# Read stage and multiply stage of a decoder layer merged into one block, with new orders on VectorE and ScalarE

## The chip, the cores and the metric

One core of a Trainium2 chip runs the whole layer. The metric is the device time of one execution in microseconds (us); three executions are shown, with their median. The engines are TensorE (PE, its weight loads PEld), VectorE (DVE), ScalarE (ACT), GpSimd (POOL) and the DMA queue of SyncE (SP).

## The reference, cut to what matters

The layer adds three parts to a state `x` of 2 x 512 tokens by 1024: a rotary attention with 4-bit weights, a "read, attend, read, multiply, write" part whose state has 4 channels for each of 256 features, and a linear layer with 4-bit weights from a table. The change lies in the second part:

```python
hidden_states = rat_write(hidden_states, attn_out, ...)      # first write
mlp_in = rat_read(hidden_states, mlp_read_w, mlp_read_g, mlp_read_b, 2)
g_in, u_in = (mlp_in[..., :H], mlp_in[..., H:])
gate = jnp.einsum('bli,oi->blo', g_in, mlp_in_w[0])
up = jnp.einsum('bli,oi->blo', u_in, mlp_in_w[1])
mlp_out = jax.nn.silu(gate) * up
hidden_states = rat_write(hidden_states, mlp_out, ...)       # second write

# rat_read: y = einsum(x, W) over the 4 channels, for each of the outputs; then a
#   normalisation over the 256 features, times gamma, plus beta
# rat_write, last line: hs * A_full + out * B_full, with
#   A_bar = exp(delta * A_neg), B_bar = (A_bar - 1) / (A_neg - SSM_EPS) * B_proj
```

## The kernel before, in words

The 1024 tokens are eight tiles of 128 (`NT` = 8), four of each batch. Nothing schedules the work but the order in which each engine's list of instructions is written, and semaphores between the engines. A block begins on all engines when the block before has ended on all of them.

`write_read` (L1990) is one block. In its first part TensorE and ScalarE make the low-rank products of the first write, while VectorE finishes the dequantiser's quarters up to `Q_MLP`. Its second part, called the **read loop** here, goes over the tiles i = 0 to 7, and each engine has its own list:

- VectorE, for tile i: `wr.update(i)` (three instructions, L1695, L1699, L1702, that make the two terms of the next state), then `rd.stats(i-1)` (mean and variance of the former tile's read, L899 and L902), then `wr.total(i)` (L1708, the sum that is the next state of the tile), at i = 2 the four instructions of `soft_sum`, then `rate(i+2)` (L1676), `skip(i+1)` (L1684) and `rd.finish(i-1)` (four small instructions from the root to the scale, L820 to L823, and two that normalise, L911).
- TensorE, for tile i: waits for `wr.new` (the end of `total(i)`), `turn_h` (eight transposes of the new state, L864), `products` (sixteen small matmuls, as profiled, on its copy in SBUF, L875), `turn_y(i-1)` (transposes of the normalised former tile, L892), and for i under 4 half a tile of the dequantised weight (`turn_half`, L1972).
- ScalarE, for tile i: `exponent(i+1)` (L1659), `root(i-1)` (L924), `copy_y(i-2)` (L930), `copy_h(i)` (two copies, L920), `copy_half` (L1982). Exponential, square root and SiLU each need another function table on ScalarE; the loads stand in the list as ACT_TABLE_LOAD under the line of the instruction that wants them.

`mlp` (its code is L1711 to L1755) is a block of its own. It has 16 steps, one for each batch and each of the 8 tiles of 128 of M. A **step** on TensorE is eight matmuls of 128x512 (four to the gate, four to `up`, L1733), on ScalarE one SiLU (L1745), on VectorE one product (L1753). Three pairs of PSUM buffers go round: step n waits for the product of step n-3. With each step go one **quarter** of the dequantiser on ScalarE (`blend`, two ACTIVATEs, L1887) and on VectorE (`merge`, L1855 to L1897), 16 quarters in all. Ahead of step 9, TensorE turns one tile of the weight in two halves (`deq.turn`, L1972), and the second waits for ScalarE's copy of the first. `write_norm_forward` is the block behind it: the second write, a normalisation and the linear layer.

Of the kernel before, what the change touches and what calls it, by code (L numbers as in the profile page):

```python
# [15 lines left out]
P = 128  # L16
# [809 lines left out]
class Read:  # L826


    def __init__(self, nc, ctx, name, h, rw, gam, bet, n_out, ident, eps, half_mask, inT, p_h, p_y, p_t, hT=None, yn=None,
# [7 lines left out]
        self.hT = hT or [sb(f"{name}hT{i}", [P, D])[:] for i in range(2)]  # L837
# [29 lines left out]
    def products(self, pe, i):  # L867
        W, ny = self.W, len(self.p_y)
        if i == 0:
            pe.wait_ge(self.made, 1)  # L870
        pe.wait_ge(self.hc, 2 * i + 2)
        if i >= ny:
            pe.wait_ge(self.yn_done, self.n_out * (i - ny + 1))
        for k in range(KT):
            ins = pe.matmul(self.p_y[i % ny][:, k // 4, (k % 4) * W:(k % 4 + 1) * W],  # L875
                            self.hT[i % 2][:, k * P:(k + 1) * P], self.wbd[:, k].rearrange("p o j -> p (o j)"),
                            start=True, stop=True)
        ins.then_inc(self.ydone, 1)
# [36 lines left out]
    def copy_h(self, act, i):  # L915
        for g in range(2):
# [3 lines left out]
            act.activation(self.hT[i % 2][:, g * 512:(g + 1) * 512], self.p_h[g][:], ACT.Copy).then_inc(self.hc, 1)  # L920
# [57 lines left out]
def read_attend(nc, a, acc, ident, ident_bf, ident_r, eps, h, mask, half_mask, ones, deq, loads, early, pos, inv, qkvT, swapT,  # L978
# [4 lines left out]
    with ExitStack() as ctx:  # L983
        sb, psum, sem = scope(nc, ctx)
        with ExitStack() as lease:
# [20 lines left out]
                  hT=[wide[:, n * D:(n + 1) * D] for n in range(2)], lent=lent,  # L1006
# [547 lines left out]

class Write:
# [33 lines left out]
    def main(self, pe, i):  # L1589
# [4 lines left out]
        for k in range(self.n_k):  # L1594
            lhs = self.sT[:, i % 2, k, :] if self.src is not None else self.srcT[:, k, i * P:(i + 1) * P]
# [115 lines left out]
def mlp(nc, inT, wT, yT, deq, fT):  # L1711

    with ExitStack() as ctx:
        sb, psum, sem = scope(nc, ctx)
        sg = [sb(f"m_sg{i}", [P, S]) for i in range(2)]
        p_g = [psum(f"m_g{i}", [P, S]) for i in range(3)]
        p_u = [psum(f"m_u{i}", [P, S]) for i in range(3)]
        done, silu, mul = sem("m_done"), sem("m_silu"), sem("m_mul")
        p_w = psum("m_pw", [P, 512])
        block = ctx.enter_context(nc.Block())  # L1720
        steps = [(b, m) for b in range(B) for m in range(MT)]
        turn_at = {9: 4}

        @block.tensor
        def _(pe):
            for n, (b, m) in enumerate(steps):
                if n in turn_at:
                    deq.turn(pe, turn_at[n], p_w)
                if n >= 3:
                    pe.wait_ge(mul, n - 2)  # L1730
                for g, dst in enumerate((p_g, p_u)):
                    for ic in range(IC):
                        ins = pe.matmul(dst[n % 3][:], wT[:, g, ic, m * P:(m + 1) * P],  # L1733
                                        inT[:, g * IC + ic, b * S:(b + 1) * S], start=ic == 0, stop=ic == IC - 1)
                ins.then_inc(done, 1)

        @block.scalar
        def _(act):
            for n in range(len(steps)):
                if n in turn_at:  # L1740
                    deq.copy(act, turn_at[n], p_w, fT)
                act.wait_ge(done, n + 1)
                if n >= 2:
                    act.wait_ge(mul, n - 1)
                act.activation(sg[n % 2][:], p_g[n % 3][:], ACT.Silu).then_inc(silu, 1)  # L1745
                for q in range(mlp_quarter(n), mlp_quarter(n + 1)):
                    deq.blend(act, q)

        @block.vector
        def _(dve):  # L1750
            for n, (b, m) in enumerate(steps):
                dve.wait_ge(silu, n + 1)
                dve.tensor_tensor(yT[:, m, b * S:(b + 1) * S], p_u[n % 3][:], sg[n % 2][:], ALU.mult).then_inc(mul, 1)  # L1753
                for q in range(mlp_quarter(n), mlp_quarter(n + 1)):
                    deq.merge(dve, q)  # L1755


# [28 lines left out]

def mlp_quarter(n):

    return Q_MLP + (Q_W2 - Q_MLP) * n // (2 * MT)


class Dequantiser:
# [152 lines left out]
    def merge(self, dve, q):  # L1945

        h, pair = q // QUARTERS, q % QUARTERS
        if pair == 0:
# [41 lines left out]
def write_read(nc, h, o_all, odT, bias_row, du, rw, gam, bet, ones, ident, eps, half_mask, inT, spread, fT, deq, fetch, early):  # L1990


    with ExitStack() as ctx:
        sb, psum, sem = scope(nc, ctx)
        p_h = [psum(f"w1ph{i}", [P, 512]) for i in range(2)]
        p_y = [psum(f"w1py{i}", [P, 2, 512]) for i in range(2)]
        p_t = [psum(f"w1pt{i}", [P, 512]) for i in range(2)]
        ab = [spread[:, n * 3 * XH:(n + 1) * 3 * XH].rearrange("p (n c) -> p n c", c=3) for n in range(2)]
        bb = [spread[:, (2 + n) * XC * XH:(3 + n) * XC * XH].rearrange("p (n c) -> p n c", c=XC) for n in range(2)]
        wr = Write(nc, ctx, "w1", h, ident, ones, odT, bias_row, du, IC, 2, [t[:] for t in p_h],  # L2000
                   [p_y[0][:, n] for n in range(2)], p_t[0], src=o_all, p_s=[p_y[1][:, n] for n in range(2)], ab=ab, bb=bb)
        rd = Read(nc, ctx, "r2", h, rw, gam, bet, 2, ident, eps, half_mask, inT, p_h, p_y, p_t,
                  hT=[spread[:, (4 + n) * D:(5 + n) * D] for n in range(2)])
        p_w = p_t[1]
        flat = wr.sp[:].rearrange("p t s -> p (t s)")
        deq.borrow(Q_W1, [flat[:, n * HALF:(n + 1) * HALF] for n in range(4)]
                   + [inT[:, n // 2, HALF * (n % 2):HALF * (n % 2 + 1)] for n in range(6)])
        chain, fetched, first = sem("w1chain"), sem("w1fetched"), sem("w1first")
        half = NT // 2
# [16 lines left out]
        def _(pe):  # L2026
            wr.turn(pe, 0)
# [13 lines left out]
            for i in range(NT + 1):  # L2041
                if i < NT:
                    pe.wait_ge(wr.new, i + 1)
                    rd.turn_h(pe, i)
                    rd.products(pe, i)
                if i >= 1:
                    rd.turn_y(pe, i - 1)
                if i < len(W1_HALVES):
                    deq.turn_half(pe, W1_HALVES[i], p_w)

        @block.scalar
        def _(act):
            for b in range(B):
# [18 lines left out]
            for i in range(NT + 2):  # L2072
# [4 lines left out]
                if 1 <= i <= NT:  # L2077
                    rd.root(act, i - 1)
                if i >= 2:
                    rd.copy_y(act, i - 2)  # L2080
                if i < NT:
                    rd.copy_h(act, i)
                if 1 <= i <= len(W1_HALVES):
                    deq.copy_half(act, W1_HALVES[i - 1], p_w, fT)

        @block.vector
        def _(dve):
            link = Chain(dve, chain)
            for q in range(Q_W1, Q_MLP):
# [6 lines left out]
            for i in range(NT + 1):  # L2096
                if i < NT:
                    wr.update(dve, i)
                if i >= 1:
                    rd.stats(dve, link, i - 1)  # L2100
                if i < NT:
                    wr.total(dve, i)
                    if i + 2 == half:
                        wr.soft_sum(dve, link, 1)
                    if i + 2 < NT:
# [3 lines left out]
                if i >= 1:  # L2109
                    rd.finish(dve, link, i - 1)  # L2110


def write_norm_forward(nc, h, acc, x1_kept, odT, bias_row, du, ones, ident, eps, fT, bias_src, out, deq):
# [3 lines left out]
    with ExitStack() as ctx:  # L2117
# [5 lines left out]
                   [t[:] for t in po[2:4]], p_l, srcT=acc)  # L2123
# [36 lines left out]
        def _(pe):  # L2160
# [11 lines left out]
            def unit(u):  # L2172
# [7 lines left out]
                for k in range(KT):  # L2180
                    ins = pe.matmul(po[u % 4][:], acc[:, k, i * P:(i + 1) * P], fT[:, k, g * 512:(g + 1) * 512],  # L2181
# [20 lines left out]
        def _(act):  # L2202
# [11 lines left out]
            def copy_z(i):  # L2214
# [141 lines left out]
def program(nc, a, out):  # L2356
    with ExitStack() as keep:
# [24 lines left out]
        with ExitStack() as ml:  # L2382
            sbm, _, _ = scope(nc, ml)
            wT, inT2 = sbm("mlp_w", [P, 2, IC, M]), sbm("inT2", [P, 2 * IC, TOK])
            with ExitStack() as w1:
                sbw, _, _ = scope(nc, w1)
                odT1, bias1, du1 = sbw("odT1", [P, IC, OD]), sbw("bias1", [1, OD - C_B]), sbw("du1", [DR + 1, XH])
                spread = acc[:, 0:6, :].rearrange("p k t -> p (k t)")
                write_read(nc, h, o_all, odT1, bias1, du1, rw2, g2, b2, ones, ident, eps, half_mask, inT2, spread, fT, deq,
# [3 lines left out]
            deq.use(Q_MLP, "dm_", ml, nc)  # L2393
            mlp(nc, inT2, wT, acc, deq, fT)
# [65 lines left out]
```

## Time and profile before

| | |
|---|---|
| median of 3 executions | 1802.5 us (1802.19 to 1802.68) |
| the profiled execution, its own time | 1804.03 us |
| its span, first to last instruction | 1802.3 us |
| busy in the span: PE, DVE, ACT, POOL | 89%, 75%, 51%, 32% |
| mean granted TensorE clock | 0.941 |
| read loop (first update of a tile to the end of the block) | 1466.8 to 1546.7 us |
| `mlp` block | 1546.7 to 1611.3 us |

The profiled execution spends 1.7 us outside its span. The shares of busy time are means over stages that have different limits; the stages that are changed are 145 us of the 1802, so only what happens between 1466 and 1611 us is read in detail. A granted clock of 0.50 is the lower of TensorE's two levels (1.2 GHz), 1.00 is the upper (2.4 GHz).

### The profile page before, as it was taken

The page shows a single profiled execution, that of the slowest core. Times are in us where ns is not written, and L with a number is a line of the kernel's source. Part 1 is how long each engine was busy: PE and PEld are TensorE (multiplying, and loading weights), DVE is VectorE, ACT ScalarE, POOL GpSimd, SP SyncE. Part 2 cuts the span into 40 slices and gives each one's busy share as a digit, 9 for nine tenths or more (in the row PEclk, how much of TensorE's full clock was granted, in tenths as well). Part 3 has the DMA queues.
Part 4 walks back from the last instruction along what each step waited for, and adds up shares of the span by engine and source line. Part 5 has one row for each costly group of instructions (what it writes and reads, how often), then busy time and mean ns, then how long its engine had stood idle before and what let it go on. Part 6 is the DMA issues. An engine that isn't in the chain of part 4 may idle for free. (4 is left out here: it accounts for less than half of the span.)

```text
span 1802.3 us, 21041 instructions
## 1 busy us (share of the span) xinstructions
PE 1595.5 (89%) x6880; PEld 1056.0 (59%) x6880; DVE 1358.9 (75%) x2078; ACT 910.2 (51%) x1682; POOL 577.8 (32%) x463
## 2 busy tenths in 40 slices
PE   4899999999999999999999988677889757888999
PEld 3466666666666666666666655465456446445444
DVE  7688788788878888888887866685578679568881
ACT  3345455555454454554555444233468876457630
POOL 2246446446446446455455454201110100000000
PEclk9999999999999999999999999887889865899999
DMA  5002102102101111111110010230644200010121
GB/s 182 24 25 59 35 24 59 36 24 59 36 25 58 35 33 51 35 37 46 36 45 26 24 35 12 79 140 30 123 84 58 91 1 0 1 35 1 47 76 41
DMA packets 30963, 84.20 MB, mean 47 GB/s; under 512 B 6006, under 2 KB 7304, under 8 KB 30600
## 3 DMA queue, kind: packets, MB, share of 16 engines
q1 hardware_dynamic: 30856, 82.87, 16.0%
q8 instruction: 56, 0.92, 0.2%
q14 instruction: 51, 0.42, 0.1%
HBM read 70.27 MB, written 12.58 MB: 46 GB/s over the span
## 5 line engine op out<-in xcount | busy, mean ns | idle before, releaser
L518 DVE SCALAR_TENSOR_TENSOR acc<-pj,sc_o,acc 128x1024 f32<-128x1024 f32 x232 | 293.8, 1278 | 89.6 <-PE pj L649 86.2
L628 POOL TENSOR_TENSOR prob<-prob,inv_total 128x512 f32<-128x512 f32 (+3 forms) x256 | 189.6, 745 | 386.0 <-DVE inv_total L560 386.0
L518 DVE SCALAR_TENSOR_TENSOR q_acc<-pj,sc_q,q_acc 128x1024 f32<-128x1024 f32 x224 | 286.2, 1278 | 34.6 <-PE pj L649 29.3
L649 PE MATMUL pj<-ctx_hi,w_o 128*128 128x512 f32 x528 | 237.1, 449 | 25.6 <-ACT spare L407 12.3
L649 PE MATMUL pj<-zT_hi,w_q 128*128 128x512 f32 x512 | 225.9, 441 | 3.7 <-PEq L81 3.1
L649 PE MATMUL pj<-ctx_lo,w_o 128*128 128x512 f32 x528 | 208.1, 394 | 0.0
L461 ACT ACTIVATE prob<-ps,low_max 128x512 f32<-128x512 f32 (+3 forms) x256 | 134.0, 526 | 144.4 <-DVE low_max L553 144.3
L649 PE MATMUL pj<-zT_lo,w_q 128*128 128x512 f32 x512 | 204.9, 400 | 0.0
L703 PE MATMUL ps<-kT,qT 128*128 128x512 f32 (+3 forms) x512 | 186.2, 446 | 10.2 <-ACT prob L461 10.2
L727 PE MATMUL pv<-probT,v 128*128 128x512 f32 (+3 forms) x512 | 169.4, 433 | 0.0
L649 PEld LDWEIGHTS pj<-ctx_hi,w_o 128*128 128x128 f32 x528 | 99.1, 188 | 110.6 <-DVE acc L518 43.0
L451 ACT ACTIVATE probT<-pt 128x512 f32<-128x512 f32 (+3 forms) x256 | 111.4, 435 | 69.5 <-PE pt L717 68.5
L553 DVE TENSOR_REDUCE low_max<-ps 128x1 f32<-128x512 f32 (+3 forms) x256 | 123.1, 481 | 28.2 <-PE ps L706 28.2
L717 PE MATMUL pt<-ident,prob 128*128 128x128 f32 x640 | 115.6, 279 | 19.0 <-ACT probT L451 9.4
L618 POOL TENSOR_TENSOR acc<-acc,spare 128x1024 f32<-128x1024 f32 x32 | 76.6, 2394 | 143.9 <-ACT spare L407 143.9
L649 PEld LDWEIGHTS pj<-zT_hi,w_q 128*128 128x128 f32 x512 | 98.2, 192 | 40.7 <-issue 21.1
L649 PE MATMUL pj<-zT_hi,w_kv 128*128 128x512 f32 x240 | 119.8, 499 | 1.8 <-DVE kv_acc L518 1.1
L703 PEld LDWEIGHTS ps<-kT,qT 128*128 128x128 f32 x512 | 94.0, 191 | 46.6 <-ACT prob L461 27.4
L717 PEld LDWEIGHTS pt<-ident,prob 128*128 128x128 f32 x640 | 74.4, 141 | 77.8 <-POOL prob L628 42.2
L2181 PE MATMUL w2po<-fT,acc 128*128 128x512 f32 x256 | 112.8, 599 | 2.2 <-ACT acc L2221 2.2
L649 PEld LDWEIGHTS pj<-ctx_lo,w_o 128*128 128x128 f32 x528 | 99.6, 189 | 16.6
L407 ACT ACTIVATE spare<-pj,sc_o 128x1024 f32<-128x1024 f32 x32 | 35.7, 1115 | 144.8 <-PE pj L649 144.8
(332 smaller groups left out, 3154.9 us busy)
## 6 DMA issues: line engine op xcount, KB each, us to landing
raw_o<-in_w_o SPq DMA_DIRECT2D x33, 512.0 KB, 3.6
raw_q<-in_w_q SPq DMA_DIRECT2D x32, 512.0 KB, 3.6
x_ring<-qk_kept SPq DMA_DIRECT2D x64, 128.0 KB, 4.7
ln_x<-in_x SPq DMA_DIRECT2D x8, 512.0 KB, 7.1
raw_kv<-in_w_k SPq DMA_DIRECT2D x8, 512.0 KB, 3.5
raw_kv<-in_w_v SPq DMA_DIRECT2D x8, 512.0 KB, 4.6
x<-in_x SPq DMA_DIRECT2D x8, 512.0 KB, 7.2
x_kept<-x SPq DMA_DIRECT2D x8, 512.0 KB, 3.5
```

Source lines behind the costliest of these rows:

```text
L407: act.activation(dst[:], pj[slot][:], ACT.Copy, scale=scale).then_inc(evac_s, 1)
L451: act.activation(probT[:, b, 0:qt + 1, qt * P:(qt + 1) * P], pt[:, 0:(qt + 1) * P].rearrange("p (k c) -> p k c", c=P), ACT.Copy).then_inc( ...
L461: act.activation(prob[:, k % PROBS, 0:w], ps[n % 2][:, 0:w], ACT.Exp, bias=low_max[:, n:n + 1], scale=-1.0, accum_out=total[:, n:n + 1]).t ...
L518: dve.scalar_tensor_tensor(out=dst, in0=pj[slot][:], scalar=scale, in1=dst, op0=ALU.mult, op1=ALU.add).then_inc(evac_v, 1)
L553: dve.tensor_reduce(low_max[:, n:n + 1], ps[n % 2][:, 0:(qt + 1) * P], AX.X, ALU.min).then_inc(max_done, 1)
L618: pool.tensor_tensor(acc[:, n, :], acc[:, n, :], spare[:], ALU.add).then_inc(spare_added, 1)
L628: pool.tensor_tensor(prob[:, k % PROBS, 0:w], prob[:, k % PROBS, 0:w], inv_total[:, n:n + 1].to_broadcast([P, w]), ALU.mult).then_inc(norm ...
L649: ins = pe.matmul(pj[slot][:, b * S:(b + 1) * S], lhs, part[:, b * S:(b + 1) * S], start=n == 0, stop=n == 1)
L703: pe.matmul(ps[n % 2][:, 0:w], qT[:, b * S + qt * P:b * S + (qt + 1) * P], kT[:, par, b * S:b * S + w], start=True, stop=False)
L717: ins = pe.transpose(pt[:, c * P:(c + 1) * P], prob[:, k % PROBS, c * P:(c + 1) * P], ident[:])
L727: ins = pe.matmul(pv[:, c * P:S], v[:, par, b * S + c * P:b * S + (c + 1) * P], probT[:, b, c, c * P:S], start=c == 0, stop=c == QT - 1)
L2181: ins = pe.matmul(po[u % 4][:], acc[:, k, i * P:(i + 1) * P], fT[:, k, g * 512:(g + 1) * 512], start=k == 0, stop=k == KT - 1)
```

## The change

1. The block `mlp` goes; its 16 steps move into the block of `write_read`.
2. Steps 0 to 3 stand inside the read loop. TensorE has step i-5 for i = 5 to 8, behind `products(i)` and ahead of `turn_y(i-1)`; ScalarE has its SiLU (`gated`) for i = 6 to 9, behind `root`; VectorE has the product at the end of i = 6, 7, 8, and that of step 3 after the loop. These four steps share one pair of PSUM buffers (`p_g`, `p_u`), so step n waits there for the product of step n-1. Steps 4 to 15 come after the loop with three pairs, two of which are the buffers of `turn_h` and `products`.
3. VectorE's list in the read loop: `total(i)` now ahead of `stats(i-1)`. ScalarE's list: `copy_y(i-2)`, `copy_h(i)`, then `root(i-1)`.
4. The dequantiser: quarter `Q_MLP` is done at the end of the read loop (`begin` and `merge(..., begun=True)` on VectorE, one `blend` on ScalarE), the other 15 with steps 4 to 15, two of them with steps 7, 11 and 15. The turn of a weight tile stands ahead of step 12, not of 9.
5. Places in SBUF and PSUM: the two buffers of the products are one bank each, the transposed state lies in a part of `fT` that is free, the working tiles of the dequantiser are borrowed, and `acc` holds the multiply stage's output by batch, with batch 1 first; later readers of it are changed alike (`by_batch`, `turned_tile`).

```diff
+def by_batch(acc):
+    return acc[:].rearrange("p (b x) (y s) -> p b (x y) s", b=B, s=S)
+def turned_tile(v, k, i):
+    return v[:, B - 1 - i // (NT // B), k, (i % (NT // B)) * P:(i % (NT // B) + 1) * P]
...
-def mlp(nc, inT, wT, yT, deq, fT):
...
+MLP_IN_READ, MLP_FROM = 4, 5
+STEPS = [(b, m) for b in range(B) for m in range(MT)]
+MLP_TURNS = {12: 4}
 def mlp_quarter(n):
-    return Q_MLP + (Q_W2 - Q_MLP) * n // (2 * MT)
+    return Q_MLP + 1 + (Q_W2 - Q_MLP - 1) * (n - MLP_IN_READ) // (len(STEPS) - MLP_IN_READ)
...
+    def begin(self, dve, h):
+        self.low_shift(dve, h)
+        self.low_bit(dve, h)
+        for n in range(3):
+            self.high_bit(dve, h, n)
...
+        p_g, p_u = psum("m_g", [P, S]), psum("m_u", [P, S])
+        gate, up = (p_g, p_h[0], p_y[0]), (p_u, p_h[1], p_y[1])
...
         @block.tensor
+            def step(n):
+                b, m = STEPS[n]
+                pe.wait_ge(rd.yc, rd.nb * NT * (b + 1) // B)
+                if n == 0:
+                    pe.wait_ge(fetched, 16 * len(fetch))
+                    pe.wait_ge(wr.dc, NT)
+                if n == MLP_IN_READ:
+                    pe.wait_ge(rd.hc, 2 * NT)
+                elif n == MLP_IN_READ + 1:
+                    pe.wait_ge(rd.yn_done, rd.n_out * NT)
+                elif n:
+                    pe.wait_ge(mul, n if n < MLP_IN_READ else n - 2)
+                k = 0 if n < MLP_IN_READ else n % 3
+                for g, dst in enumerate((gate, up)):
+                    for ic in range(IC):
+                        ins = pe.matmul(dst[k][:], wT[:, g, ic, m * P:(m + 1) * P],
+                                        inT[:, g * IC + ic, b * S:(b + 1) * S], start=ic == 0, stop=ic == IC - 1)
+                ins.then_inc(done, 1)
...
                     rd.products(pe, i)
+                if i >= MLP_FROM:
+                    step(i - MLP_FROM)
                 if i >= 1:
                     rd.turn_y(pe, i - 1)
                 if i < len(W1_HALVES):
                     deq.turn_half(pe, W1_HALVES[i], p_w)
+            for n in range(MLP_IN_READ, len(STEPS)):
+                if n in MLP_TURNS:
+                    deq.turn(pe, MLP_TURNS[n], p_w)
+                step(n)
...
         @block.scalar
+            def gated(n):
+                act.wait_ge(done, n + 1)
+                if n == 0:
+                    act.wait_ge(wr.mul_done, half)
+                if n >= 2:
+                    act.wait_ge(mul, n - 1)
+                act.activation(sg[n % 2], gate[0 if n < MLP_IN_READ else n % 3][:], ACT.Silu).then_inc(silu, 1)
...
-                if 1 <= i <= NT:
-                    rd.root(act, i - 1)
                 if i >= 2:
                     rd.copy_y(act, i - 2)
                 if i < NT:
                     rd.copy_h(act, i)
+                if 1 <= i <= NT:
+                    rd.root(act, i - 1)
+                if i > MLP_FROM:
+                    gated(i - 1 - MLP_FROM)
                 if 1 <= i <= len(W1_HALVES):
                     deq.copy_half(act, W1_HALVES[i - 1], p_w, fT)
+                if i == NT:
+                    deq.blend(act, Q_MLP)
+            for n in range(MLP_IN_READ, len(STEPS)):
+                if n in MLP_TURNS:
+                    deq.copy(act, MLP_TURNS[n], p_w, fT)
+                gated(n)
+                for q in range(mlp_quarter(n), mlp_quarter(n + 1)):
+                    deq.blend(act, q)
...
         @block.vector
+            def product(n):
+                b, m = STEPS[n]
+                if n == 0:
+                    dve.wait_ge(wr.st, NT)
+                if n == MT:
+                    dve.wait_ge(wr.new, NT)
+                dve.wait_ge(silu, n + 1)
+                dve.tensor_tensor(yT[:, B - 1 - b, m, :], up[0 if n < MLP_IN_READ else n % 3][:], sg[n % 2],
+                                  ALU.mult).then_inc(mul, 1)
...
             for i in range(NT + 1):
                 if i < NT:
                     wr.update(dve, i)
-                if i >= 1:
-                    rd.stats(dve, link, i - 1)
+                if i == NT:
+                    dve.wait_ge(wr.new, NT)
+                    deq.begin(dve, Q_MLP // QUARTERS)
                 if i < NT:
                     wr.total(dve, i)
                     if i + 2 == half:
                         wr.soft_sum(dve, link, 1)
+                if i >= 1:
+                    rd.stats(dve, link, i - 1)
+                if i < NT:
                     if i + 2 < NT:
                         wr.rate(dve, i + 2)
                     if i + 1 < NT:
                         wr.skip(dve, i + 1)
                 if i >= 1:
                     rd.finish(dve, link, i - 1)
+                if i > MLP_FROM:
+                    product(i - 1 - MLP_FROM)
+            deq.merge(dve, Q_MLP, begun=True)
+            product(MLP_IN_READ - 1)
+            for n in range(MLP_IN_READ, len(STEPS)):
+                product(n)
+                for q in range(mlp_quarter(n), mlp_quarter(n + 1)):
+                    deq.merge(dve, q)
```

## Rows read from the trace of the kernel before

**Rows 1.** Busy time by stretch: length, PE, PEld, DVE, ACT, POOL, clock, DMA.

```profile
1510.40:1519.00 8.60, 6.52 (x29) 5.70 (x28) 7.87 (x17) 6.78 (x11) 0.00 (x0) 0.50 0.01 2
1562.00:1579.20 17.20, 17.20 (x41) 7.41 (x39) 12.93 (x21) 10.00 (x15) 0.00 (x0) 1.00 0.00 0
```

**Rows 2.** Waits in the read loop: us in total, times, longest us.

```profile
PE w1ph L864 <- DVE h L1708: 19.9, 8, 10.3
ACT r2sd L924 <- DVE r2mv L902: 17.9, 8, 4.8
```

**Rows 3.** VectorE's timeline in the read loop: start us, us, instruction, idle before.

```profile
1468.55 1.22 DVE L1702 TENSOR_TENSOR acc<-acc,w1od 128x1024 f32<-128x1024 f32 x1
1469.87 1.23 DVE L1708 TENSOR_TENSOR h<-h,acc 128x1024 f32<-128x1024 f32 x1
...
1506.24 0.76 DVE L899 BATCH_NORM_STATS2 r2st<-w1py 128x6 f32<-128x256 f32 x2 [0.52 <-PE w1py L875]
...
1507.20 1.19 DVE L1708 TENSOR_TENSOR h<-h,acc 128x1024 f32<-128x1024 f32 x1
...
1509.63 0.16 DVE L820 RECIPROCAL r2r<-r2sd 128x2 f32<-128x2 f32 x1
...
1510.44 0.99 DVE L911 TENSOR_SCALAR r2yn<-w1py,r2mv,r2t 128x256 f32<-128x256 f32 x2
1511.36 0.95 DVE L1695 SCALAR_TENSOR_TENSOR acc<-acc,w1nb 128x768 f32<-128x768 f32 x1
...
1514.82 0.76 DVE L899 BATCH_NORM_STATS2 r2st<-w1py 128x6 f32<-128x256 f32 x2 [0.51 <-PE w1py L875]
```

**Rows 4.** ScalarE's timeline in the read loop, tiles 5 and 6.

```profile
1511.56 1.28 ACT L1659 ACT_TABLE_LOAD   x1
1512.86 0.84 ACT L1659 ACTIVATE acc<-acc 128x768 f32<-128x768 f32 x1
...
1515.90 0.29 ACT L924 ACTIVATE r2sd<-r2mv,eps 128x2 f32<-128x2 f32 x1 [0.90 <-DVE r2mv L902]
1516.10 1.49 ACT L930 ACTIVATE inT<-w1pt,b,g 128x128 f32<-128x128 f32 x4
...
1519.03 0.60 ACT L920 ACTIVATE acc<-w1ph 128x512 f32<-128x512 f32 x1 [0.26 <-PE w1ph L864]
```

**Rows 5.** ScalarE's timeline in the block after `mlp`.

```profile
1675.92 0.39 ACT L1633 ACTIVATE w2od<-w2po 128x256 f32<-128x256 f32 x1 [0.78 <-PE w2po L1610]
1676.33 1.28 ACT L2205 ACT_TABLE_LOAD   x1
```

**Rows 6.** TensorE's timeline in the read loop and in `mlp`.

```profile
1517.03 1.97 PE L864 MATMUL w1ph<-ident,h 128*128 128x128 f32 x8 [1.39 <-DVE h L1708]
...
1523.15 1.06 PE L892 MATMUL w1pt<-ident,r2yn 128*128 128x128 f32 x4
...
1546.75 3.43 PE L1733 MATMUL m_g<-inT,mlp_w 128*128 128x512 f32 x4 [1.85 <-PEq L1993]
...
1551.73 1.88 PE L1733 MATMUL m_g<-inT,mlp_w 128*128 128x512 f32 x4
...
1562.03 1.88 PE L1733 MATMUL m_g<-inT,mlp_w 128*128 128x512 f32 x4
...
1577.48 1.88 PE L1733 MATMUL m_u<-inT,mlp_w 128*128 128x512 f32 x4
...
1582.43 1.88 PE L1733 MATMUL m_g<-inT,mlp_w 128*128 128x512 f32 x4
```

**Rows 7.** ScalarE's and VectorE's timelines behind the last step.

```profile
1606.66 0.60 ACT L1745 ACTIVATE m_sg<-m_g 128x512 f32<-128x512 f32 x1 [1.43 <-PE m_u L1733]
1607.16 1.51 ACT L1887 ACTIVATE dm_t<-dm_t,d_lut,d_step 128x512 f32<-128x512 int32 x2
...
1607.29 0.69 DVE L1753 TENSOR_TENSOR acc<-m_u,m_sg 128x512 f32<-128x512 f32 x1 [1.29 <-ACT m_sg L1745]
...
1610.28 0.73 DVE L1897 COPY_PREDICATED d_w<-dm_t 128x512 f32<-128x512 int32 x1
```

More of the change, by code:

```diff
@@ L836, in __init__ @@
         self.wbd = sb(name + "wbd", [P, KT, n_out, 32])
-        self.hT = hT or [sb(f"{name}hT{i}", [P, D])[:] for i in range(2)]
+        self.hT = hT or [sb(f"{name}hT{i}", [P, 2, 512])[:] for i in range(2)]
         self.yn = yn or [sb(f"{name}yn{i}", [P, n_out * XH])[:] for i in range(2)]
@@ L1708, in total @@
         dve.tensor_tensor(hv, hv, self.bb[i % 2], ALU.add).then_inc(self.new, 1)
-def mlp(nc, inT, wT, yT, deq, fT):
[L1713 to L1755, printed above, removed]
 HALF = D // 2
@@ L1943, in merge_one, with merge @@
             self.keep_all(dve, h)
-    def merge(self, dve, q):
+    def begin(self, dve, h):
[3 more added lines that the diff above has]
+            self.high_bit(dve, h, n)
+    def merge(self, dve, q, begun=False):
         h, pair = q // QUARTERS, q % QUARTERS
-        if pair == 0:
+        if pair == 0 and not begun:
             if q in STAGES:
@@ L1987, in copy, with write_read @@
             self.copy_half(act, 2 * o + g, pt, fT)
-def write_read(nc, h, o_all, odT, bias_row, du, rw, gam, bet, ones, ident, eps, half_mask, inT, spread, fT, deq, fetch, early):
+def write_read(nc, h, o_all, odT, bias_row, du, rw, gam, bet, ones, ident, eps, half_mask, inT, acc, wT, fT, deq, fetch, early):
     with ExitStack() as ctx:
         sb, psum, sem = scope(nc, ctx)
+        spread = acc[:, 0:4, :].rearrange("p k t -> p (k t)")
         p_h = [psum(f"w1ph{i}", [P, 512]) for i in range(2)]
-        p_y = [psum(f"w1py{i}", [P, 2, 512]) for i in range(2)]
-        p_t = [psum(f"w1pt{i}", [P, 512]) for i in range(2)]
+        p_y = [psum(f"w1py{i}", [P, 512]) for i in range(2)]
+        p_t, p_w = psum("w1pt", [P, 512]), psum("w1pw", [P, 512])
+        p_g, p_u = psum("m_g", [P, S]), psum("m_u", [P, S])
@@ L2005, in write_read @@
+        gate, up = (p_g, p_h[0], p_y[0]), (p_u, p_h[1], p_y[1])
+        yT = by_batch(acc)
         flat = wr.sp[:].rearrange("p t s -> p (t s)")
+        old = wr.od[:].rearrange("p t s -> p (t s)")
+        sg = [old[:, n * S:(n + 1) * S] for n in range(2)]
         deq.borrow(Q_W1, [flat[:, n * HALF:(n + 1) * HALF] for n in range(4)]
                    + [inT[:, n // 2, HALF * (n % 2):HALF * (n % 2 + 1)] for n in range(6)])
+        deq.borrow(Q_MLP, [flat[:, n * HALF:(n + 1) * HALF] for n in range(4)]
+                   + [old[:, n * HALF:(n + 1) * HALF] for n in range(2, 8)])
@@ L2008, in write_read @@
         chain, fetched, first = sem("w1chain"), sem("w1fetched"), sem("w1first")
+        done, silu, mul = sem("m_done"), sem("m_silu"), sem("m_mul")
         half = NT // 2
```

30 lines of the change are left out of this document (14 added, 16 removed).

## The prediction, made before the changed kernel was run

> **What bounds the kernel now.** The page's busy shares say TensorE (89%), but they are means; the change touches only the read loop and the multiply block, so I read the busy time by stretch there first. It shows two regimes. In the read loop VectorE is the busy engine (7.87 of 8.60 us), ScalarE has 6.78, and TensorE, at the lower clock, still has 2.1 us idle in each tile. In the multiply block TensorE is busy without a gap at the upper clock [rows 1]. So moving steps from the second stage into the gaps of the first looks like a gain. Four steps are worth 3.43 us each at the upper clock: 10.30 us for three, 1551.73 to 1562.03 [rows 6].
>
> Second, the waits in the read loop: TensorE waits for the new state of a tile (19.9 us), and ScalarE's root waits for the statistics (17.9 us) [rows 2]. Third, VectorE's timeline gives the loop's period: statistics start at 1506.24 and again at 1514.82, so 8.58 us, of which only 0.51 are idle and end with TensorE's products [rows 3]. The ring that ends last is: sum of the next state, transposes, copy by ScalarE, products, statistics, next sum.
>
> **The change: the order in the read loop.** With the sum ahead of the statistics the ring above is cut, and VectorE's own list is left. Its pieces, start to start, are [rows 3]: statistics 0.96 (1506.24 to 1507.20); sum, rate and skip 2.43 (to 1509.63); reciprocal to normalising 0.81; normalising 0.92 (to 1511.36); update 2.95 (to 1514.31, where the idle 0.51 begins). Together 8.07. Add 0.10, because the sum now stands right behind the multiply that it needs (1468.55 + 1.22 = 1469.77 against 1469.87). That would be 8.17 us a tile, a gain of 0.4.
>
> But the reciprocal needs the root, and the root now stands behind `copy_h(i)` on ScalarE. The second copy begins 2.00 us after the transposes of its tile and lasts 0.60 (1517.03 and 1519.03) [rows 4, 6]. Then the root's function table has to be loaded, as the exponential has used ScalarE since. Before, this 1.28 us load stood right behind the exponential, in ScalarE's idle time. Is it put directly ahead of its user, or moved up by whoever places it? The next block answers: ScalarE there was idle 0.78 us, waiting for a copy's input, and the square root's load came only behind that copy (1675.92, 1676.33) [rows 5]. I take it that the same holds here: load 1.28, gap 0.02, root 0.29 [rows 4].
>
> So the new ring, from one tile's transposes to the next: copies 2.60, load 1.30, root and hand-over 0.35, to the normalising 0.81, 0.92, update and gap 3.05, sum 1.19, and 0.06 to the transposes: **10.28 us against 8.58**. The new state is early only in name: it is made behind `finish` of the former tile, which is late by the load. Tiles 3 to 4 and 4 to 5 lose 1.70 each. At the first tiles I take 0.4 in all, between nothing and 1.7 each: VectorE waited 2.3 us for the first products there, and at tile 2 the four instructions of `soft_sum` cover the load. Tile 5's transposes come at 1517.03 + 3.8 = 1520.8.
>
> A rule of the Trainium skill speaks against this part, in "ScalarE: Activation LUTs", sections "What ACT_TABLE_LOAD costs" and "Table sets: the hidden batching unit": calls are to be grouped by table set, and each switch is to be budgeted at some 2.66 us, a load of 1283 ns and a drain of 1380 ns. The trace agrees on the load alone: it ends at 1512.84, and the exponential starts at 1512.86 [rows 4]. By the page's drain the six loads that I find exposed below would add an estimated 8 us more to the sum; I go by the row.
>
> **Steps 0 to 3 inside the loop.** What does a step take there? At the start of `mlp` the first gate group of four matmuls took 3.43 us at the lower clock, and the next step began 4.98 us after the first [rows 6]. Steps at the upper clock take 3.43, a whole step at the lower clock would be twice the first group, 6.9. The read loop ran at 0.50 throughout [rows 1], so each step begins low; I take 5.0 and keep 3.4 and 6.9 as bounds.
>
> Round 5 (tile 5's transposes to tile 6's): transposes and products occupy TensorE for 6.12 (1517.03 to 1523.15), step 0 5.0, `turn_y` 0.86 (an estimate: its 1.06 less the overlap with what follows): 12.0. The ring's 10.28 lies inside it.
>
> Round 6: `turn_y(4)` stood behind the step, so ScalarE's `copy_y(4)` (1.49) comes now, ahead of `copy_h(6)`; the copies end 2.75 after the transposes began. Load of the root's table to 4.05, root to 4.38, table load for SiLU to 5.68, SiLU 0.60, product 0.69 [rows 7] to 7.05. Only then may step 1 start, as the four steps share one pair of buffers: TensorE has been through with its products since about 6.4. Step 5.0, `turn_y` 0.86: 12.9.
>
> The last round has tile 7 and, behind it, the end of the loop. Step 2 again starts at 7.05 and ends at 12.05, `turn_y(6)` is done at 13.1, and only then do `copy_y(6)`, the load, root 7, the load for SiLU, SiLU and the product follow one another: 1.5 + 1.3 + 0.3 + 1.3 + 0.6 + 0.7 = 5.7, with hand-overs 18.95. Step 3 and `turn_y(7)`: 24.8. Queued behind root 7 on VectorE are `finish(7)`, the product and quarter `Q_MLP`; `begin` of that quarter fits in the wait.
>
> So step 4 starts at 1520.8 + 12.0 + 12.9 + 24.8 = 1570.5. Before, it started at 1562.03 [rows 6]: **+8.5**. The six exposed loads are those of rounds 3 and 4, two in round 6, two at the end; that of round 5 lies beside the step.
>
> **Steps 4 to 15.** Twelve at 3.43 as before: nothing. VectorE now has 15 quarters in twelve steps. A quarter and its product took VectorE 12.93 us busy in five steps [rows 1], 2.6 a step; 15/12 of the quarters keep it under 3.43, and three buffers bridge the double ones. If that cover fails, each double costs up to 1.4. The turn ahead of step 12 comes behind step 11, which has two quarters on ScalarE: TensorE's second half waits for a copy behind four blends, not two. The turn cost 3.23 before (1577.48 to 1582.43 less 1.72); two blends more are 1.4 (1.51 less an overlap) [rows 6, 7]: **+1.4**, between 0 and 3. The last step too has two quarters instead of one; behind it the block ended 4.35 us after the SiLU's start (1606.66 to 1611.01), now two blends later: **+1.4**.
>
> **At nothing:** the block boundary before `mlp` goes, but what it held, `turn_y` and the copy, is counted above. No DMA is moved; SP's and GpSimd's lists keep their place. The new places in `acc`, `fT` and PSUM keep every instruction's shape. The later readers of `acc` only step by 512 instead of 1024 elements; I know no row for that, bounds 0 and 0.5.
>
> **Sum:** 8.5 + 1.4 + 1.4 = +11.3. The profiled execution has 1804.0 (span 1802.3 and 1.7 around), so it would be 1815.3. The median of the runs is 1.5 lower: **1813.8 us**, slower by 0.6%. About 0.2%, 3.6 us, is what the measurement can tell from no change.
>
> **Rivals.**
> - *TensorE stays at the lower clock through steps 0 to 3.* For it: 0.50 throughout a loop in which TensorE was busy three quarters of the time. Against it: the dense matmuls raised it within one group at 1546.75. Each step has 1.9 more, and step 4 starts low: 4 x 1.9 + 1.6 = +9: 1823.
> - *The clock rises with step 0 and stays.* Steps at 3.43, round 5 then limited by the ring at 10.3, rounds 6 and last 11.1 and 20.9 by the same sum: step 4 at 1563.1, +1.0, with the two 1.4 1806.3. For it: TensorE's gaps shrink. Against it: it idles before each step for the SiLU.
> - *The table load is moved up ahead of the copies.* The ring is then 8.98, with the root still behind `copy_h`, and the loads in round 6 and at the end vanish: step 4 at about 1560, 1803.4, no difference. Against it: [rows 5].
> - *The steps fit into the shadow* (the other side). If step, SiLU and product lay wholly beside the ring, tile "8" would be reached at 1520.8 + 3 x 10.28 = 1551.6, 10.4 us before the old start of step 4, and with 2.8 given back the time is 1794.9. It decides when the three rounds take less than 38.4 us together, not 49.7. Against it: the shared pair of buffers and `turn_y` behind the step.
>
> **How the numbers follow.** Forecast (steps partly low) 0.57; all low 0.16; clock stays up 0.12; load moved up 0.08; shadow 0.07. 1806.3 sits near the bound, so half of that case counts as no change: faster 0.07, same 0.13, slower 0.80. The range leaves out the shadow, the load and a part beyond the lower clock's case: 1804 to 1823.
>
> **What would show it.** In the profile after: the root's table load behind L920's copies, with VectorE's reciprocal idle some 2 us for ScalarE in each of tiles 3 to 5, and transposes 10.3 apart; TensorE idle before steps 1 to 3, the longest before step 3 (some 6 us); step 4 at about 1570; a stall of 4.6 us at the turn; the next block at about 1622. Wrong would be: transposes 8.2 to 8.6 apart (the load hidden), steps of 3.4 or 6.9 us in the loop, or step 4 before 1562.

## The result and the profile after

The changed kernel takes 1814.2 us (median of 4 executions, 1812.09 to 1815.37) against 1802.59 before: ratio 1.0055, 95% interval 1.0037 to 1.0073. It is slower by 0.6%; 1813.8 was forecast. In a second comparison (e9) the same two kernels gave 1819.1 and 1803.36, ratio 1.0074 (1.0054 to 1.0093).

The profiled execution took 1813.46 us (span 1811.8). I measure from the first transposes of the read loop, those of tile 0, as the stages ahead of them, which the change leaves alone, end at different times: first transposes at 1471.15 us before, 1467.40 after, and between 1465.24 and 1475.88 in all fourteen profiles of this study. This is TensorE's timeline after, with its transposes at L864 and its steps at L2025; it answers to [rows 6]:

```profile
1467.40 1.97 PE L864 MATMUL w1ph<-ident,h 128*128 128x128 f32 x8 [10.28 <-DVE h L1718]
...
1506.99 1.97 PE L864 MATMUL w1ph<-ident,h 128*128 128x128 f32 x8 [2.23 <-DVE h L1718]
...
1517.27 1.97 PE L864 MATMUL w1ph<-ident,h 128*128 128x128 f32 x8 [3.08 <-DVE h L1718]
1519.92 3.67 PE L875 MATMUL w1py<-r2wbd,fT 128*128 128x64 f32 x16 [0.69 <-ACT fT L920]
1523.39 2.93 PE L2025 MATMUL m_g<-inT,mlp_w 128*128 128x512 f32 x4
1526.16 1.88 PE L2025 MATMUL m_u<-inT,mlp_w 128*128 128x512 f32 x4
1527.88 0.60 PE L892 MATMUL w1pt<-ident,r2yn 128*128 128x128 f32 x4
1528.31 1.04 PE L864 MATMUL w1ph<-ident,h 128*128 128x128 f32 x8
...
1535.45 3.74 PE L2025 MATMUL m_g<-inT,mlp_w 128*128 128x512 f32 x4 [1.76 <-DVE acc L2123]
...
1541.18 1.04 PE L864 MATMUL w1ph<-ident,h 128*128 128x128 f32 x8
...
1548.25 3.75 PE L2025 MATMUL m_g<-inT,mlp_w 128*128 128x512 f32 x4 [2.34 <-DVE acc L2123]
1551.80 2.33 PE L2025 MATMUL m_u<-inT,mlp_w 128*128 128x512 f32 x4
1553.97 0.60 PE L892 MATMUL w1pt<-ident,r2yn 128*128 128x128 f32 x4
1560.52 3.75 PE L2025 MATMUL m_g<-inT,mlp_w 128*128 128x512 f32 x4 [5.95 <-DVE acc L2123]
1564.06 3.02 PE L2025 MATMUL m_u<-inT,mlp_w 128*128 128x512 f32 x4
1566.92 0.60 PE L892 MATMUL w1pt<-ident,r2yn 128*128 128x128 f32 x4
1567.36 3.60 PE L2025 MATMUL w1ph<-inT,mlp_w 128*128 128x512 f32 x8
...
1591.39 3.60 PE L2025 MATMUL w1py<-inT,mlp_w 128*128 128x512 f32 x8
1594.83 0.60 PE L1946 MATMUL w1pw<-ident,d_w 128*128 128x128 f32 x4
1598.97 0.66 PE L1946 MATMUL w1pw<-ident,d_w 128*128 128x128 f32 x4 [3.55 <-ACT fT L1956]
1599.47 1.88 PE L2025 MATMUL m_g<-inT,mlp_w 128*128 128x512 f32 x4
...
1619.48 7.72 PE L1606 MATMUL w2po<-odT,acc 128*128 128x376 f32 x16 [6.12 <-PEq L1967]
```

Read down the starts of L864: 1506.99 to 1517.27 is tile 4, 10.28 us. Then come the four steps, each with a wait for VectorE's product ahead of it but the first: 1.76 us before step 1, 2.34 before step 2, 5.95 before step 3. Step 4 begins at 1567.36.

ScalarE in tile 4, and at the end of the loop; it answers to [rows 4]:

```profile
1508.99 0.60 ACT L920 ACTIVATE fT<-w1ph 128x512 f32<-128x512 f32 x1 [0.26 <-PE w1ph L864]
1509.61 1.28 ACT L924 ACT_TABLE_LOAD   x1
1510.90 0.29 ACT L924 ACTIVATE r2sd<-r2mv,eps 128x2 f32<-128x2 f32 x1
...
1554.61 1.50 ACT L930 ACTIVATE inT<-w1pt,b,g 128x128 f32<-128x128 f32 x4 [7.22 <-PE w1pt L892]
1556.13 1.28 ACT L924 ACT_TABLE_LOAD   x1
1557.42 0.29 ACT L924 ACTIVATE r2sd<-r2mv,eps 128x2 f32<-128x2 f32 x1
1557.74 1.28 ACT L2067 ACT_TABLE_LOAD   x1
1559.03 0.60 ACT L2067 ACTIVATE w1od<-m_g 128x512 f32<-128x512 f32 x1
```

The load stands between copy and root. VectorE waits for the root. Its timeline in tile 4, and at the end of the loop (normalising, then the product of step 2):

```profile
1511.23 0.17 DVE L820 RECIPROCAL r2r<-r2sd 128x2 f32<-128x2 f32 x1 [1.98 <-ACT r2sd L924]
...
1558.78 0.99 DVE L911 TENSOR_SCALAR r2yn<-w1py,r2mv,r2t 128x256 f32<-128x256 f32 x2 [0.27 <-DVE r2t L823]
1559.69 0.68 DVE L2123 TENSOR_TENSOR acc<-m_u,w1od 128x512 f32<-128x512 f32 x1
```

The waits between 1466 and 1568 us:

```profile
ACT inT L930 <- PE w1pt L892: 27.9, 8, 7.2
DVE r2r L820 <- ACT r2sd L924: 22.9, 7, 5.8
...
PE m_g L2025 <- DVE acc L2123: 10.1, 3, 6.0
```

Against [rows 2] the wait has turned round: ScalarE's root waited 17.9 us in all for VectorE's statistics, now VectorE waits 22.9 for the root.

### The profile page after: what moved, and what is told of

It is laid out like the page before. It is cut to its first block and busy times, and to the rows that moved or that the text cites. A ratio compares the mean times of both kernels' runs of the same rounds, so it can differ in the third digit from the quotient of the medians.

```text
span 1811.8 us, 21054 instructions
## 1 busy us (share of the span) xinstructions
PE 1594.8 (88%) x6880; PEld 1052.9 (58%) x6880; DVE 1358.0 (75%) x2078; ACT 915.6 (51%) x1686; POOL 578.8 (32%) x463
## 5 line engine op out<-in xcount | busy, mean ns | idle before, releaser
L649 PEld LDWEIGHTS pj<-ctx_lo,w_o 128*128 128x128 f32 x528 | 99.6, 189 | 16.4
```

The costliest lines, as they stand in the source:

```text
L649: ins = pe.matmul(pj[slot][:, b * S:(b + 1) * S], lhs, part[:, b * S:(b + 1) * S], start=n == 0, stop=n == 1)
```

## The experiments

Twelve kernels ran. Single executions scatter by several us on those chips (the kernel before: most between 1798 and 1811), and the ratios compare with the kernel before only, so each experiment is compared with the changed kernel by its profile: "stretch" is the time from the first transposes to the start of the next block, "tile 5" and "step 4" are counted from the first transposes too. Each stretch is that of one execution. Two kernels were profiled twice: the changed one differed by 1.5 us (e9), the best one by 0.2 (e11), so a difference under some 1.5 us is not told apart here.

| kernel | tile 5 | tile 6 | tile 7 | step 4 | stretch | median us | ratio to before (95%) |
|---|---|---|---|---|---|---|---|
| before | 45.88 | 54.45 | 63.02 | 90.88 | 140.18 | 1802.59 | |
| changed | 49.87 | 60.91 | 73.78 | 99.96 | 152.08 | 1814.2 | 1.0055 (1.0037 to 1.0073) |
| e1 root first | 43.17 | 56.32 | 67.23 | 90.22 | 144.04 | 1806.99 | 1.0021 (1.0000 to 1.0043) |
| e2 old orders | 45.29 | 55.73 | 67.77 | 89.00 | 142.81 | 1811.48 | 1.0030 (1.0014 to 1.0046) |
| e3 preload | 45.62 | 57.04 | 69.37 | 90.91 | 144.72 | 1809.64 | 1.0030 (1.0011 to 1.0048) |
| e4 orders only | 49.68 | 59.96 | 70.24 | | 147.45 | 1811.32 | 1.0027 (1.0008 to 1.0046) |
| e5 turn_y first | 49.87 | 60.82 | 72.77 | 89.19 | 143.95 | 1808.28 | 1.0027 (1.0009 to 1.0044) |
| e6 even quarters | 49.88 | 61.19 | 74.18 | 100.46 | 147.41 | 1811.06 | 1.0040 (1.0024 to 1.0056) |
| e7 no SiLU | 49.87 | 60.99 | 73.74 | 94.68 | 148.48 | 1813.5 | 1.0049 (1.0034 to 1.0064) |
| e8 best | 45.87 | 57.19 | 66.60 | 82.83 | 129.78 | 1795.33 | 0.9938 (0.9918 to 0.9958) |
| e9 changed again | 49.71 | 61.66 | 74.98 | 101.51 | 153.63 | 1819.1 | 1.0074 (1.0054 to 1.0093) |
| e10 before, turn split | 45.88 | 54.46 | 63.04 | 90.93 | 139.14 | 1803.24 | 0.9999 (0.9987 to 1.0011) |
| e11 best again | 45.90 | 57.40 | 66.82 | 83.06 | 130.01 | 1793.45 | 0.9942 (0.9920 to 0.9964) |
| e12 best, sum first | 43.14 | 56.38 | 65.06 | 83.12 | 130.08 | 1792.56 | 0.9929 (0.9913 to 0.9946) |

**e1, the root first.**

```diff
+                if 1 <= i <= NT:
+                    rd.root(act, i - 1)
                 if i >= 2:
                     rd.copy_y(act, i - 2)
                 if i < NT:
                     rd.copy_h(act, i)
-                if 1 <= i <= NT:
-                    rd.root(act, i - 1)
```

> Of the changed kernel, only ScalarE's list in the read loop is put back: the root of the former tile ahead of the two copies; VectorE keeps the sum ahead of the statistics, the steps stay in the loop. My theory (the root with its table load behind the copies sets the ring): VectorE no longer waits 2 us for the root; but the copies of a tile now come behind root and copy_y, some 1.3 us late, so TensorE's list (transposes, late products, turn_y, half turn) limits tiles 3 and 4 to 9.2 and 8.4 us; the product of step 0 and 1 comes 1.5 us earlier, that of step 2 some 3 us; in all about -9 us on the changed kernel, 1805. Rival (the steps in the loop alone set the time, the lists do not matter): 1814, no difference from the changed kernel. Rival (late copies cost as much as the load): 1811 to 1814.

The stretch fell by 8.0 us. Tile 5 came 6.7 sooner, tile 5 to 6 took 13.2 instead of 11.0: the late copies exist, but cost less than the root's place. VectorE, no longer waiting, began its sums 8.17 and 8.18 us apart (1490.78, 1498.95, 1507.13), where the prediction had put its own list at 8.17.

**e2, both lists old.** e1's edit, and `rd.stats(dve, link, i - 1)` ahead of `wr.total(dve, i)` again.

> The changed kernel with both lists put back (VectorE: statistics ahead of the sum; ScalarE: root ahead of the copies); the steps, the turn and the quarters stay as changed. My theory: transposes 8.6 us apart up to tile 5 as before the change, then steps as in the changed kernel with the product earlier: about -8.5 us, 1805.5, still some 3 us slower than before the change, which is the price of the steps' place and of the double quarters. Rival (moving the steps is what costs, the orders are free): 1813 to 1814. Rival (moving the steps is a gain and only the orders hide it): under 1799.

The stretch fell by 9.3 us, so the orders are not free, and the steps with the rest of the change are still 2.6 us dearer than before it. Step 4 came 1.9 us sooner than before the change; what is behind it gave that back and more (see e6).

**e3, the load alone.** The sharpest test: nothing is taken away, one tiny instruction per tile is added (`warm` is a new tile for its unused result).

```diff
+                if 1 <= i <= NT:
+                    act.activation(warm[:, i:i + 1], eps[:], ACT.Sqrt)
                 if i >= 2:
                     rd.copy_y(act, i - 2)
```

> The changed kernel with one more instruction per tile: a square root of one element per partition on ScalarE, directly ahead of copy_y and copy_h, its result unused. It changes nothing but where the root's table load stands. My theory (the load behind the copies costs 1.3 us in each tile that it is exposed in): transposes of tiles 3 to 5 come 9.0 us apart instead of 10.3, and six exposed loads less in all: -7.8 us, 1806.5. Rival (the root's place behind the copies costs, not the load): 1813 to 1815. Rival (VectorE's list is the bound anyway): 1813 to 1815.

ScalarE's timeline of e3, from the end of tile 4 (its transposes began at 1503.15) to the root in tile 5 (1512.02):

```profile
1508.60 1.28 ACT L2095 ACT_TABLE_LOAD   x1
1509.90 0.20 ACT L2095 ACTIVATE warm<-eps 128x1 f32<-128x1 f32 x1
1510.38 1.51 ACT L930 ACTIVATE inT<-w1pt,b,g 128x128 f32<-128x128 f32 x4 [0.28 <-PE w1pt L892]
1513.17 0.60 ACT L920 ACTIVATE fT<-w1ph 128x512 f32<-128x512 f32 x1 [1.29 <-PE w1ph L864]
1514.02 0.60 ACT L920 ACTIVATE fT<-w1ph 128x512 f32<-128x512 f32 x1 [0.26 <-PE w1ph L864]
1514.52 0.29 ACT L924 ACTIVATE r2sd<-r2mv,eps 128x2 f32<-128x2 f32 x1
```

The load has moved into idle time, the root follows the copy at once, and tile 4 takes 8.87 us (36.75 to 45.62 behind the first transposes), not 10.28. Step 4 came 9.05 us sooner, the stretch is 7.4 shorter; the whole kernel makes 40 table loads, as the changed one does. Only their place differs.

**e4, the orders without the overlap.**

```diff
-MLP_IN_READ, MLP_FROM = 4, 5
+MLP_IN_READ, MLP_FROM = 0, NT + 2
...
-                elif n:
+                elif n > 2:
                     pe.wait_ge(mul, n if n < MLP_IN_READ else n - 2)
...
-            product(MLP_IN_READ - 1)
```

> The changed kernel with no step inside the read loop: both new lists stay, all 16 steps come behind the loop in the same block with three pairs of buffers, one quarter with each, the turn ahead of step 12. It is the reorder without the overlap. My theory: transposes 10.3 us apart from tile 3 to tile 7, the first step some 33.7 us after tile 5's transposes; the overlap of four steps gained only about 1 us, and no double quarters give back 2.8: about -4 us on the changed kernel, 1810. Rival (the steps in the loop are what costs): 1803 or less. Rival (the overlap is worth its four steps, 10 us or more): 1820 or more.

147.45, so the orders, in the merged block, cost 7.3 us against before, 3.8 of them by tile 5 and 7.2 by tile 7, and putting four steps into this loop brought no gain: with the orders as changed the overlap is a loss of 4.6, turn and quarters included. e4 makes 36 table loads, as many as the kernel before, so it is not their number that costs.

**e5, turn_y ahead of the step.**

```diff
-                if i >= MLP_FROM:
-                    step(i - MLP_FROM)
                 if i >= 1:
                     rd.turn_y(pe, i - 1)
+                if i >= MLP_FROM:
+                    step(i - MLP_FROM)
```

> The changed kernel with one edit on TensorE: turn_y of the former tile ahead of the step instead of behind it. My theory (copy_y waits behind the step, and with it root, both table loads, SiLU and product, worst in the last round): tile 5 to tile 6 about 11.5 us instead of 11.0, tile 6 to tile 7 11.1 instead of 12.9, tile 7 to step 4 18 instead of 26.2; about -9.5 us on the stretch from the first transposes to the next block (152.1 us in the changed kernel), 1804.6. Rival (the shared pair of buffers sets the rounds, wherever turn_y stands): less than 2 us gained, 1812 to 1814.

The stretch fell by 8.1 us with one swapped pair of lines. Tile 7 to step 4 took 16.4 us instead of 26.2. Tile 6 to 7 gained only 0.9 of the expected 1.8: step 1 ran for 5.8 us instead of 5.3, and `turn_y` now waited 1.4 us for VectorE's normalised tile.

**e6, turn and quarters evened.**

```diff
-MLP_TURNS = {12: 4}
+MLP_TURNS = {11: 8, 12: 9}
...
-    return Q_MLP + 1 + (Q_W2 - Q_MLP - 1) * (n - MLP_IN_READ) // (len(STEPS) - MLP_IN_READ)
+    return Q_MLP + (1, 2, 4, 5, 6, 8, 9, 10, 12, 13, 14, 15, 16)[n - MLP_IN_READ]
...
-                    deq.turn(pe, MLP_TURNS[n], p_w)
+                    deq.turn_half(pe, MLP_TURNS[n], p_w)
```

(and `copy_half` for `copy` on ScalarE)

> The changed kernel with the turn's first half ahead of step 11 and its second ahead of step 12, and the doubled quarters at steps 5, 8 and 11, so that the last step has one. The read loop is not touched. My theory (the turn and the doubled last quarter cost 1.4 us each, and most of the turn's stall is the wait for the first half's copy): the stall of 4.6 us becomes about 1, the next block starts 1.4 us sooner behind the last step: -5 us on the stretch, 147.1; 1809. Rival (VectorE has no room for 15 quarters in 12 steps): the stall comes back as waits of TensorE for products, under 1 us gained.

```profile
1595.95 0.60 PE L1946 MATMUL w1pw<-ident,d_w 128*128 128x128 f32 x4
1596.39 3.60 PE L2025 MATMUL w1py<-inT,mlp_w 128*128 128x512 f32 x8
1599.83 0.60 PE L1946 MATMUL w1pw<-ident,d_w 128*128 128x128 f32 x4
```

TensorE's timeline of e6, with one step between the halves of the turn: no bracket, no wait. The turn costs twice 0.44 us instead of 4.65; the stretch fell by 4.7 in all.

**e7, no SiLU.** `ACT.Copy` in place of `ACT.Silu` in `gated`.

> The changed kernel with SiLU replaced by a plain copy: the SiLU is left out of the result. It takes away SiLU's table loads and with them the root's in the last two tiles, nothing else. My theory (two exposed loads in round 6 and two at the end): -1.3 in tile 6 to tile 7, where TensorE's products then end last, -1.5 in tile 7 to step 2, -2.6 behind step 2: about -5.4 us, stretch 146.7, 1809. The loads of tiles 3 to 5 stay and transposes stay 10.3 apart. Rival (the loads lie beside TensorE's steps there): under 1 us.

Step 4 came 5.3 us sooner, near the 5.4 expected, but by other parts: 0.1 in tile 6 to 7, 1.7 from tile 7 to step 2, 2.2 from step 2 to step 3, 1.4 from step 3 to step 4. Of these, 2.2 us are steps 2 and 3 themselves, which took 4.93 and 5.03 us instead of 5.72 and 6.40 and were not in my sum; the waits gave 3.1. VectorE's timeline of e7 in tile 6 shows why the first is so small:

```profile
1533.43 0.99 DVE L911 TENSOR_SCALAR r2yn<-w1py,r2mv,r2t 128x256 f32<-128x256 f32 x2
1534.35 0.68 DVE L2123 TENSOR_TENSOR acc<-m_u,w1od 128x512 f32<-128x512 f32 x1
```

The product stands behind `finish(5)` in VectorE's list, and that waits for the root, whose load is still there in this tile. With the SiLU ready 1.4 us earlier the product starts only 0.3 us sooner (1534.35 with the transposes at 1528.33; 1534.62 with 1528.31 in the changed kernel), and TensorE still waits 1.56 us for it. In the next two rounds the root's load is gone as well, since no SiLU has changed the table, and there the gain is. The stretch shows only 3.6 us less, since the turn and the step behind it took 1.7 us more (below).

**e8, the version these point to**: the edits of e2, e5 and e6 together.

> The version that the runs so far point to: steps 0 to 3 in the read loop with VectorE's and ScalarE's old lists, turn_y ahead of the step, the turn in two halves at steps 11 and 12, the doubled quarters at 5, 8 and 11. My theory: 45.3 us to tile 5 as before the change, then 10.5, 9.9 and 16.3 to step 4, 41.2 for twelve steps, 1 for the turn, 4.9 to the next block: stretch 129 us against 140.2 before the change and 152.1 with it; 1792, faster than both. Rival (what is won is only moved to the dequantiser's chain behind the loop): 1799 to 1803.

129.78 us where 129 was expected, and 0.9938 of the kernel before (0.9918 to 0.9958). It makes 40 table loads, four more than the kernel before.

**e9 to e12**, timed in five rounds on one chip.

> The changed kernel once more, beside the three below on one chip, so that they are compared with it and not only with the kernel before. Expected: stretch from the first transposes to the next block 152 us within 0.5, as it is made only of instructions' durations; the stages ahead of it, which the change does not touch, may differ by some us from one execution to the next, as they did so far (first transposes between 1465.2 and 1475.8 us in ten profiles); 1814 to 1816.

153.63: off by 1.5. Tiles 1 to 5 agree within 0.2; the rest is in the three rounds behind tile 5, where the steps took 5.4, 5.8, 6.0 and 6.5 us (4.5, 5.3, 5.7, 6.4 in the first profile).

The edit of e10: `turn_at = {9: 4}` becomes `{9: 8, 10: 9}` in `mlp`, with `turn_half` and `copy_half`.

> The kernel before the change with one edit: the dequantiser's turned tile in two halves, ahead of step 9 and ahead of step 10, instead of both ahead of step 9. It asks what the even turn is worth without any of the change. My theory: the 3.2 us stall becomes about 0.9 (two groups of four transposes and no wait), -2.3 us: stretch 137.9 against 140.2, 1801. Rival (the wait only moves to the weight's quarter that is merged late): no difference.

Only 1.0 us less, and no difference in the times. TensorE's timeline of e10:

```profile
1585.17 0.66 PE L1972 MATMUL m_pw<-ident,d_w 128*128 128x128 f32 x4 [1.04 <-DVE d_w L1897]
1585.67 1.88 PE L1733 MATMUL m_g<-inT,mlp_w 128*128 128x512 f32 x4
1587.39 1.88 PE L1733 MATMUL m_u<-inT,mlp_w 128*128 128x512 f32 x4
1589.11 0.60 PE L1972 MATMUL m_pw<-ident,d_w 128*128 128x128 f32 x4
```

The wait for the copy is gone, but ahead of step 9 the weight's last quarter is still being merged: 1.04 us idle. I had overlooked that part of the stall; the rival had it.

> The version with the old lists, turn_y ahead of the step and even quarters once more, timed in five rounds beside the others. Expected: stretch 129.8 within 1, some 8 to 10 us under the kernel before and 8 under the kernel before with the split turn, which is then the worth of four steps inside the loop.

> The same version with VectorE's new list (sum ahead of the statistics), ScalarE's old one. It asks whether the sum's place is a gain once nothing else of the change is in its way. My theory: tile 5 comes at 43.2 us instead of 45.9, but the copies of tile 5 come behind root and copy_y, so tile 5 to tile 6 takes 13.2 instead of 11.3: stretch 129, within 1 us of the old list. Rival (the sum ahead is worth its 2 to 3 us): 127 or less. Rival (it is a loss in itself): 132 or more.

130.01 and 130.08. With the sum first, tile 5 comes 2.8 us sooner (43.14 against 45.90), and tile 5 to 6 takes 13.2 us instead of 11.5; and 1.9 more go between tile 7 and step 2, which took 8.0 us instead of 6.1. In both places ScalarE's copies again come behind root and `copy_y`: TensorE waits 2.56 us for them in tiles 5 and 7, against 0.69 and 0.74 in e11. The sum's place is no gain and no loss here; the two intervals overlap.

## Why the prediction was right, point by point

- **The ring of 10.28 us a tile**: measured 10.28 (1506.99 to 1517.27), with VectorE idle 1.98 for the root. That the load stays directly ahead of its user, argued from [rows 5], is shown by the profile after and by e3. Tile 5 was late by 3.99 us against the first transposes, 3.8 forecast. The 0.4 for the first tiles was 0.6, but by luck: the early sum brought tile 1 1.6 us sooner (7.04 against 8.64), and a load exposed behind it, with VectorE idle 2.38 for the first root, cost 2.0 (10.58 against 8.57); tile 2 to 3 cost 0.2. In e3 tile 1 to 2 took 9.15, so 1.4 of the 2.0 is the load. Neither part was worked out.
- **The Trainium skill's 2.66 us a switch** ("ScalarE: Activation LUTs", section "What ACT_TABLE_LOAD costs"): its load of 1283 ns agrees with the 1.28 us of the trace. No drain of 1380 ns shows where it would cost: after, the copy ends at 1509.59, the load stands from 1509.61 to 1510.89 and the root starts at 1510.90. The warning pointed the right way, but the number of switches did not decide here: e4 and the kernel before make 36 loads and differ by 7.3 us in the stretch, and e8, the fastest, makes 40. What costs is a load that somebody waits for.
- **Rounds**: 11.04, 12.87, 26.18 us against 12.0, 12.9, 24.8; together 50.1 against 49.7. The waits stand where they were said to: 1.76 us before step 1, 2.34 before step 2, 5.95 before step 3. That `turn_y`, `copy_y` and root hold up the product is shown by e5 (the place of `turn_y`, 8.1 us). The last links were told as root, SiLU's load, SiLU, product, with two exposed loads in round 6. But the product also stands behind `finish`, and the two paths end almost together: in the last round SiLU ended at 1559.63 and the normalising at 1559.77. So SiLU's own load is nearly hidden (0.3 us in round 6 of e7); what it costs is the reload that it forces on the next root. The time of 7.05 us to step 1 was right (7.14 measured) as both paths are about as long.
- **The size of a step**: 5.0 was taken, between 3.4 and 6.9. The four took 4.49, 5.29, 5.72 and 6.40: mean 5.5. It is the term that was least well sized. The last round was 1.4 too cheap by step 3. Round 5 was 1.0 too dear, 0.5 by step 0 and 0.4 by `turn_y`, which took 0.43 from start to start instead of 0.86, at the upper clock.
- **Turn**: 1599.47 is 8.08 us behind step 11's start, 1591.39, so a stall of 4.65 (4.6 said), +1.4. **Double last quarter**: +1.4 (9.71 us from the last step's start to the next block against 8.30). e6 takes both away. The steps 4 to 11 and 12 to 15 start 3.43 us apart, as before, so that the term put at nothing there was right.
- **Sum**: the stretch grew by 11.9 us, 11.3 forecast. Behind it the next block and the end took 192.3 us instead of 191.0, a term that I did not have. Most of it is the first group of that block, 7.72 us instead of 6.89, more of it at the lower clock. It goes with the doubled last quarter: in the seven kernels that have it TensorE sat idle 6.12 us ahead of this group, which then took 7.72 to 8.32; in the seven others it sat idle 4.71, and the group took 6.89 to 6.99, but 7.43 in e4 and 7.45 in e10, which stays open. e6, which alters only the turn and the quarters, has 6.92. So that quarter has a second price of some 1 us. Ahead of the stretch the profiled execution was 3.75 us quicker, in stages that did not change. So the agreement of the medians to 0.4 us is closer than the working deserves.
- **The rivals**: the clock neither stayed up nor down. "The steps fit into the shadow" was right about what is possible: e8 has tile 5 to step 4 in 37.0 us, under the 38.4 named as the point that decides, though by other lists than the change's. Of the two things named against it, `turn_y` behind the step counted: from 50.1 us, e5 alone comes to 39.3, the old lists alone (e2) to 43.7. The shared pair of buffers, the other, was kept in all runs with steps in the loop and not tested.

What each part costs, by stretches against before: the orders in the merged block +7.3 (e4), the steps with turn and quarters +2.6 (e2), both together +11.9; the 2.0 that the two leave over is near what a repeat differs by. With the old lists, `turn_y` ahead and even quarters, the merged block with its four steps in the loop is worth 9.1 us (e11 against e10).

## What to carry to other kernels

An instruction moved behind others on ScalarE takes its table load with it: before swapping two calls, look at which table the one before leaves, and who waits for the one that switches. If its place must stay, a one-element call of the same function placed where ScalarE idles takes the load out of the way (e3). When independent work is put into a loop's gaps, put it behind everything that another engine waits for; on TensorE that one swap, of `turn_y` and step, was worth 8.1 us of a loss of 11.9. Where one engine's work is handed over in halves that wait for a copy, put other work between the halves, and check that the first is ready.

## What the runs showed of the hardware that was not expected

- The granted clock in a mixed stretch was 0.75 (TensorE busy 10.44 of 13.90 us), and the same list of instructions gave other clocks in another execution: step 0 took 4.49 us in one profile of the changed kernel and 5.39 in another. Two windows of the profile after, tile 4 and the round with step 1; behind the window's length stand PE, PEld, DVE, ACT and POOL busy with their counts, then the granted clock (0.50 is the lower level throughout, 0.75 a mix):

```profile
1506.99:1517.27 10.28, 6.51 (x29) 5.71 (x29) 8.02 (x17) 6.89 (x11) 0.00 (x0) 0.50 0.00 0
1527.30:1541.20 13.90, 10.44 (x43) 6.54 (x42) 8.98 (x21) 5.94 (x10) 0.00 (x0) 0.75 0.00 0
```

- The turn's stall of about 4.6 us had a second price. In e1, e2, e3, e5 and e7 the step behind it took 4.8 to 5.7 us instead of 3.43, most of its first group at the lower clock; in the two profiles of the changed kernel it took 3.43, behind a stall of about the same length. Why it differs is open. TensorE's timeline of e2:

```profile
1592.26 0.60 PE L1946 MATMUL w1pw<-ident,d_w 128*128 128x128 f32 x4
1596.40 0.76 PE L1946 MATMUL w1pw<-ident,d_w 128*128 128x128 f32 x4 [3.54 <-ACT fT L1956]
1596.95 3.52 PE L2025 MATMUL m_g<-inT,mlp_w 128*128 128x512 f32 x4
1600.31 1.88 PE L2025 MATMUL m_u<-inT,mlp_w 128*128 128x512 f32 x4
```

- The same unchanged stages ended up to 10.6 us apart (first transposes from 1465.24 to 1475.88), nearly as much as the stretch grew by the change (11.9). The spread is already there at ScalarE's first copy of the second attention's context, 1315.0 to 1323.8 us. What makes it was not tried.
